# Value products in runs of four units instead of two, and the projections of the next batches moved away from the runs, in a 16-head cross attention

## What is computed

```python
def proj(x, W, b):
    y = x @ W.T + b
    return y.reshape(bs, -1, HEADS, D_K).transpose(0, 2, 1, 3)
qh, kh, vh = proj(q, Wq, bq), proj(k, Wk, bk), proj(v, Wv, bv)
scores = jnp.einsum('bhqd,bhkd->bhqk', qh, kh) / jnp.sqrt(jnp.asarray(D_K, jnp.float32))
attn = jax.nn.softmax(scores, axis=-1)
out = jnp.einsum('bhqk,bhkd->bhqd', attn, vh)
concat = out.transpose(0, 2, 1, 3).reshape(bs, -1, D_MODEL)
return concat @ Wo.T + bo
```

## Time and profile before

| | us |
|---|---|
| median of 3 runs | 5829.42 (5827.53 to 5834.3) |
| the profiled execution, its own time | 5833.64 |
| its span, first to last instruction | 5831.9 |
| PE busy | 5276.3 (90%) |
| DVE busy | 3851.6 (66%) |
| ACT busy | 3100.1 (53%) |
| POOL busy | 1589.2 (27%) |

### The profile page before, as it was taken

One profiled execution on the slowest core, in us unless ns is written; L12 is line 12 of the kernel. 1 busy time (PEld: TensorE's weight loads), 2 busy tenths in 40 slices (PEclk: granted clock), 3 DMA queues, 4 the chain that ended last, 5 costly groups with the idle time before them and its releaser, 6 DMA issues. The chain is left out here.

```text
span 5831.9 us, 109941 instructions
## 1 busy us (share of the span) xinstructions
PE 5276.3 (90%) x39878; PEld 3466.6 (59%) x39878; DVE 3851.6 (66%) x10948; ACT 3100.1 (53%) x4492; POOL 1589.2 (27%) x1360
## 2 busy tenths in 40 slices
PE   6999999997959999999999988979458999999996
PEld 4666666665835555555555547857355666666663
DVE  5666666665766766766766657756466676767674
ACT  3666666664624444444444445634145666666664
POOL 3222222221442222222222214500352222222220
PEclk9999999998979999999999998989578999999998
DMA  3323333332233323333332315479223232323230
GB/s 86 77 67 77 70 75 78 71 72 60 58 87 91 82 72 78 82 76 74 82 79 71 82 40 108 77 198 252 82 91 77 68 76 67 77 67 78 67 72 13
DMA packets 160603, 475.40 MB, mean 82 GB/s; under 512 B 34721, under 2 KB 85724, under 8 KB 159867
## 3 DMA queue, kind: packets, MB, share of 16 engines
q1 hardware_dynamic: 148738, 449.69, 32.5%
q0 software_dynamic: 11328, 18.72, 1.1%
HBM read 237.66 MB, written 19.88 MB: 44 GB/s over the span
## 5 line engine op out<-in xcount | busy, mean ns | idle before, releaser
L692 DVE CUSTOM_DVE_ANT_0 a_dump<-a_max,a_mqf 100x482 f32<-100x482 f32 (+1 forms) x1536 | 978.5, 657 | 426.5 <-PE a_max L883 395.6
L1635 PE MATMUL a_max<-a_stack,a_qblk 96*128 96x482 f32 (+1 forms) x2304 | 1030.4, 449 | 28.7 <-DMA a_stack<-a_khi 17.6
L1473 DVE CUSTOM_DVE_ANT_0 a_dump<-a_max,a_penq 128x482 f32<-128x482 f32 (+3 forms) x1248 | 783.0, 655 | 409.1 <-PE a_max L1635 386.9
L1466 DVE TENSOR_REDUCE a_mx<-a_max 128x1 f32<-128x482 f32 (+3 forms) x1248 | 779.6, 654 | 406.6 <-PE a_max L1635 283.4
L565 ACT ACTIVATE a_probs<-a_scores 128x800 f32<-128x800 f32 (+1 forms) x768 | 643.2, 838 | 657.4 <-PE a_scores L900 657.2
L1368 ACT ACTIVATE a_probs<-a_scores,a_kbias 128x800 f32<-128x800 f32 (+1 forms) x768 | 697.3, 926 | 404.1 <-PE a_scores L1662 404.1
L1662 PE MATMUL a_scores<-a_qblk,a_stack 128*128 128x400 f32 (+1 forms) x3072 | 832.9, 353 | 40.6 <-POOL a_qblk L1283 34.0
L1370 ACT ACTIVATE a_probs<-a_scores 128x800 f32<-128x800 f32 (+1 forms) x768 | 624.7, 836 | 410.0 <-PE a_scores L1662 406.0
L883 PE MATMUL a_max<-a_stack,a_qblk 96*100 96x482 f32 (+1 forms) x1536 | 712.1, 485 | 39.5 <-DVE a_mx L692 27.6
L1674 PE MATMUL a_pv<-a_probs,a_v_aug 128*32 128x200 f32 x12288 | 705.7, 341 | 3.0 <-ACT a_probs L1368 2.1
L1662 PEld LDWEIGHTS a_scores<-a_qblk,a_stack 128*128 128x128 f32 (+1 forms) x3072 | 548.3, 184 | 185.0 <-POOL a_qblk L1283 57.6
(11 more groups left out here) (554 smaller groups left out, 8473.0 us busy)
## 6 DMA issues: line engine op xcount, KB each, us to landing
a_stack<-a_khi SPq DMA_DIRECT2D x768, 180.5 KB, 3.3
a_ctxT<-in_ctxT_dram SPq DMA_DIRECT2D x128, 722.0 KB, 14.3
a_stack<-a_klo SPq DMA_DIRECT2D x384, 180.5 KB, 3.5
f_wb<-weights_by_token SPq DMA_DIRECT2D x16, 1600.0 KB
a_ctxn<-in_ctxn_dram SPq DMA_DIRECT2D x32, 704.0 KB
a_mt_i<-in_mask1T_dram SPq DMA_DIRECT2D x32, 600.0 KB, 6.9
a_mq_i<-in_mask_dram SPq DMA_DIRECT2D x32, 564.1 KB
a_mask_i<-in_mask_dram SPq DMA_DIRECT2D x32, 541.5 KB
```

Source lines behind the costliest of these rows:

```text
L692: nc.vector.tensor_tensor_reduce(dump[:, k % 2, 0:n], src, mqf[:, b % 2, o:o + n], 1.0, -3.0e38, ALU.mult, ALU.max, out_).then_inc(mx_free, 1)
L1466: nc.vector.tensor_reduce(out_, src, AX.X, ALU.max).then_inc(mx_free, 1)
L1473: nc.vector.tensor_tensor_reduce(dump[0:rows, k % 2, 0:n], src, penq[0:rows, b % 2, o:o + n], 1.0, -3.0e38, ALU.add, ALU.max, out_).then_i ...
L1635: pe.matmul(to[:, 0:n], qblk[0:96, b % 2, at:at + D], stack[0:96, b % 2, g, o:o + n], start=True, stop=True).then_inc(mx_full, 1)
```

## The change

The value products are issued in runs of four units (TOGETHER = 4, so NP = 6 buffers of `probs`), at u = 1, 5, 9, 13, 17, 21, for the units u-5 to u-2: the newest unit in a run is two units old instead of one. The maxima run 27 jobs ahead (PACKED_UNITS = 18) instead of 24. The copies of a finished half (`pv_evac`) come a unit later. The fixed units move: the last steps of b-1 to 5, 9, 13; `left` to 9, 13, 17; queries to 17; and the projections to units two away from every run, `v01` to 11, `k0` to 15, `k12` to 19 and `v2` to 23. The orders of POOL and SP are as before.

```diff
 PACKED = 3
 LEFT = 4 * S - PACKED * D
 MAX_JOBS = 2 * PACKED * NCH
-PACKED_LEAD = 3 * LEAD // 2
-LEFT_AT = (8, 12, 16)
-TOGETHER = 2
+PACKED_UNITS = 18
+PACKED_LEAD = 3 * PACKED_UNITS // 2
+LEFT_AT = (9, 13, 17)
+TOGETHER = 4
...
-        OUT_AT, CONCAT_AT, WO_AT, NEG1_AT, Q_AT, NEG0_AT = 2, 5, 8, 9, 18, 21
-        V01_AT, V2_AT, K0_AT, K12_AT = 9, 11, 13, 15
+        OUT_AT, CONCAT_AT, WO_AT, NEG1_AT, Q_AT, NEG0_AT = 5, 9, 13, 9, 17, 21
+        V01_AT, K0_AT, K12_AT, V2_AT = 11, 15, 19, 23
...
-                    if u == 1 and b > 0:
+                    if u == 2 and b > 0:
                         pv_evac(b - 1, 1)
-                    if u == KT + 1:
+                    if u == KT + 2:
                         pv_evac(b, 0)
...
-                    if u % TOGETHER == 0 and (b > 0 or u > 0):
-                        for back in range(TOGETHER, 0, -1):
+                    if u % TOGETHER == 1 and (b > 0 or u > 1):
+                        for back in range(TOGETHER + 1, 1, -1):
                             at = UNITS * b + u - back
                             pv_mm(at // UNITS, at % UNITS)
```

More of the change, by code:

```diff
@@ L1136, in take_max @@
                 take(mx_turn, job)
-        for g in range(LEAD):
+        for g in range(PACKED_UNITS):
             for k in range(3 * g // 2, 3 * (g + 1) // 2):
```

## The result

The change takes 6183.56 us, the median of four runs (6170.83 to 6198.83), against 5831.6 us for the kernel before on the same chips: 1.0607 times as long, with a 95% interval of 1.0588 to 1.0626. The profiled execution took 6170.83 us, 337 us more than that of before (5833.64). The forecast was +216 us, to 6050 us, with a range up to 6160: the direction and the place were right, the size was too small, and the time lies above the range.

The account below looks back on a forecast made before the run. PE, busy nearly throughout, bounds the kernel, with POOL's equally long chain holding each batch's first scores after the change. 60 x (2.86 + 0.8) - 4 = 216 us on 5833.64 gave 6050 us, range 5920 to 6160.

Parts of the forecast that it names:

- part 1: In PE's runs: six fewer a batch, 0.33 us each beyond its products, saving 1.98 us a batch.
- part 3: From a batch's first scores, s(0), to unit 19's, s(19): 34.26 us before, 30.18 after savings, plus 1.13 of slot waits.
- part 4: After PE's wait at the next batch's first scores: the clock's fall costs 0.8 us a batch, bounds 0 and 1.6.
- Part 2: From unit 19's scores to the next batch's first: `k12`'s chain over ACT and POOL takes 12.29 us, 5.81 more.
- the ring: In the longer stretch without a run: three banks may fill while DVE does maxima, some 2 us as upper bound.
- the slots: Between runs: scores wait for slots held by exponentials and by `v01` and `k0` copies, 1.13 us a batch together.
- that the clock falls in every batch: Rival, after the wait at each batch's first scores: 1.6 us lost every batch, 6097 us; chance 0.17.
- part 5: Remaining effects, -4 us together; keys' transfers queued on SP behind `v2` in unit 23 are hidden or cost up to 1 us a batch.
- That runs could pay where the chain is hidden: Rival, PE stays the bound from s(19) to s(0): POOL is hidden, 123 us gained, 5711 us; chance 0.08.

Follow-up runs that it names:

- the moved turns and queries with runs of two: The change with runs of two at odd units, a unit later than before, each projection in the unit before a run: 5762.72 us.
- the turns: The kernel with runs of two a unit later, its two turns of negated maxima moved away from the runs (units 10 and 20): 5803.61 us.
- the filled kernel: The change with 14 extra matmuls of 400 columns before the first scores of each batch, ahead of the wait for POOL: 6082.81 us.
- all projections early: The change with all four projections earlier but two units from every run (v01 3, v2 7, k0 11, k12 15): 5909.13 us.

## Why the prediction was wrong

The path, by medians: 5830 before; -68 for the moved turns and queries with runs of two; +71 for runs of four instead; +75 for projections two units from a run instead of just before one; +274 for the same projections later, `k12` in 19 and `v2` in 23, to 6184. Of the last, 101 us are the clock.

Two steps failed: the gain of fewer runs, which part 1 books and part 3 carries into the batch, and the size of the clock's loss in part 4. The profiled executions differ by 337 us, 121 more than forecast (the medians by 352).

**Part 1, the gain of fewer runs, did not come.** Its 0.33 us for each entry and exit is right: 0.34 by the turns, and the four units of 4.81 us would have taken 4.61 without their waits, against 4.93. But the step went from "12 runs become 6" to "1.98 us saved a batch" as if PE were held by nothing else between runs. The units behind a run go on at DVE's and ACT's pace, since three banks and two slots hold PE back, and what the array saves turns into small waits. The forecast booked -1.65 in s(0) to s(19); between runs of two and of four the runs show +71 us, 1.2 a batch, of which the cast held by POOL may be 28 us, as estimated above.

**Part 2, the chain, was right.** 12.29 worked out, 12.54 measured in a0 and, in the same chain in a3, 12.4. The wait is 2.7 us in a0 and 2.5 in a3 (3 to 3.7 forecast), with 1.1 and 0.9 at the slot of `k12` ahead of it.

**Part 3, the rest of the batch, came out too small, and by the ring rather than by the slots.** Without a low clock s(0) to s(19) is 622.54 - 590.32 = 32.2 us in a0, against 31.3 worked out. In a3 it is 33.5, by the filled kernel; there it was 35.1 before, not 34.26, and the same working would have given 32.2. That is 0.9 and 1.3 us, about 65 us of the 121 that were missing. The slots were not under-priced: in the batch that starts at 590.32 the two stretches in which scores wait for the slots of `v01` and `k0` are longer by 0.31 and 0.44 us, 0.75 together, where 1.13 was forecast. What was missing is small waits for DVE. An example is the two maxima behind each of the three `left`, which take 0.65 us instead of 0.44 while DVE works without a stop. PE, then DVE:

```profile
605.57 0.81 PE L1636 MATMUL a_max<-a_stack,a_qblk 96*128 96x482 f32 x2
606.22 0.53 PE L1663 MATMUL a_scores<-a_qblk,a_stack 128*36 128x400 f32 x2
...
605.18 2.35 DVE L1467 TENSOR_REDUCE a_mx<-a_max 64x1 f32<-64x480 f32 x4 [1.73 <-PE a_max L1650]
```

The prediction's bound of some 2 us beside the 1.13, "if the ring of three banks also fills", held in a0 (32.2 - 30.18 = 2.0); in a3 it was 2.4, counted from its own 35.1.

**Part 4, the clock, was too small by half.** 0.8 us a batch forecast, 1.7 measured. The price of one fall was read from a feed-forward block, 1.6 us, and is 2.6 here (47.32 against 44.72): PE's densest work follows, 6.8 us of it at half speed. And it came in most batches of a0 and nearly all of a3, not in every second. That is the other 54 us.

The rivals: that the clock falls in every batch (called the third in part 4, it stands second) was the nearest, at 6097 us. The keys' transfers of part 5, "up to 1 us a batch", cost the change almost nothing by themselves (3.2 us in 23 batches) and 3.2 us a batch once POOL's chain was shortened. That runs could pay where the chain is hidden (5711 us) did not show: with the chain hidden and each projection right before a run, runs of four give 5834.

## What to carry to other kernels

Before fewer, longer blocks of one kind are counted as a gain, look at what the other engines do during one. With few buffers they stand idle through it, and hold the fast engine right behind it. A job that moves later takes its whole chain with it, so add up its copies and what stands behind it in each engine's fixed order, up to the next thing that waits. Look too at what it now runs beside: here a moved POOL instruction held a short one on DVE. And a wait of PE that comes once in each period is to be priced with what the clock does after it: filling it with useless work was worth 101 us.

## What the runs showed of the hardware

The granted clock stayed at 1.00 with waits of 0.8 and 0.4 us in each batch of 42 us (`k12` in 17) and of 1.1 us in each of 42.3 us (all projections early), and fell to 0.50 for 6.8 us behind waits of 2.5 to 2.7 us in most batches. In the change's a0 equal waits of 2.69 us were followed by 44.7 us batches at 1.00 and by 47.3 us batches at 0.93, often by turns; what decides between them stays open. The Trainium skill, "TensorE: Matmul & The Clock Gate", "Terms", takes the penalty as the throttled time times 1 - K/N, here, as an estimate, 6.8 x 0.5 = 3.4 us. The batch lost 2.6: from its first run to the scores of unit 5 it took 7.25 us (636.45 to 643.70) instead of 4.34, and 0.35 us of waiting for the keys' transfers in unit 6 were gone in return.

A small instruction on DVE can be held by a long one on POOL. The cast of 7 columns, 0.17 us by itself, lasted 0.8 and 1.85 us in a0, and 0.44 and 1.48 in a3, where it began during POOL's 3.30 us low part of the keys (runs of four with `k12` in 16, and the kernel before with `k12` in 17). In 48 batches of the one and 46 of the other it ended 0.02 to 0.04 us after the low part. DVE's reductions out of PSUM were not held: one of 0.65 us ran at 601.97, beside POOL's 600.34 to 603.64.
